# One launch of a four-layer graph transformer: two more norms tile by tile, a sixth region for expert weights, second norm statistics on ScalarE

## What is computed

```python
# layer 0, feed-forward: 64 soft-slot experts, one slot each
x = x + _L0_ffn_ref(_layernorm(x), phi, scale, w1, b1, w2, b2)      # w1 64x768x192, w2 64x192x768, combine at the end
xn = _layernorm(x)                                                  # "combine norm"
# layer 1: graph part with the edge counts as adjacency and degrees; attention from xn
x = x + _L1_gnn_ref(xn, edge_index, W, b) + _L1_mix_ref(xn, kqv_w, ...)
# layer 2, feed-forward
x = x + gelu(x @ mlp_w1 + mlp_b1) @ mlp_w2 + mlp_b2
xm = _ln(x, ln2_g, ln2_b)                                           # "mlp norm"
logits = xm @ gate_w.T + gate_b                                     # router, top 2 of 4 experts
# layer 3, attention projection, then the router and 8 experts
y = xn + x_attn @ W_proj + b_proj
x = x + gnn + (y - mean(y)) * rsqrt(var(y) + eps) * gamma + beta
logits = x @ Wg
```

## Time and profile before

| | |
|---|---|
| median of 3 runs | 2898.76 us (2897.23 to 2898.79) |
| the profiled execution | 2899.39 us, its span 2897.3 us |
| PE busy | 2711.2 us, 94% of the span |
| DVE, ACT, POOL busy | 49%, 39%, 24% |
| PE waiting for expert weights of layer 0 (`w1`, `w2`) | 29.5 us in 11 waits, 20.3 us in 13 waits |
| PE waiting for `norm` of a `LinearNorm` | 14.5 us in 6 waits, 7.7 us the longest |
| PE waiting for `norm` of the last projection | 7.3 us, once |

### The profile page before, as it was taken

The page is one execution under the profiler, slowest core; times in us unless marked ns, Lnnn a source line. Parts: engine busy times, 40 slices in busy tenths (PEclk is TensorE's granted clock), DMA queues, the critical chain, the costliest instruction groups (busy, mean ns, idle before and its releaser), DMA issues. The chain is left out here.

```text
span 2897.3 us, 49066 instructions
## 1 busy us (share of the span) xinstructions
PE 2711.2 (94%) x20003; PEld 2467.0 (85%) x20003; DVE 1418.9 (49%) x3603; ACT 1128.7 (39%) x2103; POOL 706.7 (24%) x261
## 2 busy tenths in 40 slices
PE   9999999998678999998899999999998999999899
PEld 9999999995337988998897999999668897797699
DVE  9777465664104135548752552241665563303743
ACT  7633255561003212327731253332563432356331
POOL 0144311110002331220224433323303431113032
PEclk9999999998898999999999999999999999999999
DMA  2022221015992211221021122222001221111022
GB/s 66 12 77 80 88 72 39 29 50 223 413 380 70 71 44 34 66 86 47 12 77 45 60 77 77 68 75 77 28 1 39 67 66 49 44 34 34 23 66 71
DMA packets 164572, 220.08 MB, mean 76 GB/s; under 512 B 21801, under 2 KB 144325, under 8 KB 164350
## 3 DMA queue, kind: packets, MB, share of 16 engines
q1 hardware_dynamic: 164350, 216.95, 22.6%
HBM read 215.00 MB, written 1.92 MB: 75 GB/s over the span
## 5 line engine op out<-in xcount | busy, mean ns | idle before, releaser
L58 PE MATMUL ps<-weights_r,buf_r 128*125 128x256 f32 (+3 forms) x4110 | 545.7, 285 | 5.8 <-DVE kv L2830 1.7
L279 POOL TENSOR_TENSOR weights_r<-weights,head_weights_r 128x1536 fp32r<-128x1536 f32 (+2 forms) x80 | 276.2, 3453 | 1040.2 <-ACT head_weights_r L272 1007.8
L58 PEld LDWEIGHTS ps<-weights_r,buf_r 128*125 128x125 f32 (+1 forms) x4110 | 516.3, 187 | 9.1 <-issue 4.2
L279 POOL TENSOR_TENSOR weights_r<-weights,weights_r 128x1536 fp32r<-128x1536 f32 x76 | 269.5, 3545 | 974.0 <-ACT weights_r L272 974.0
L58 PE MATMUL ps<-xT_r,weights_r 128*128 128x376 f32 (+4 forms) x2028 | 333.8, 309 | 0.0
L58 PE MATMUL ps<-head_weights_r,buf_r 128*125 128x256 f32 (+2 forms) x2250 | 309.8, 284 | 0.0
L58 PEld LDWEIGHTS ps<-xT_r,weights_r 128*128 128x128 f32 (+1 forms) x2028 | 303.2, 189 | 3.2 <-issue 2.2
L58 PEld LDWEIGHTS ps<-head_weights_r,buf_r 128*125 128x125 f32 x2250 | 287.5, 188 | 0.0
L58 PE MATMUL ps<-weights_r,xT_r 128*125 128x256 f32 x1680 | 233.4, 282 | 8.2 <-issue 4.8
L58 PEld LDWEIGHTS ps<-weights_r,xT_r 128*125 128x125 f32 x1680 | 212.9, 186 | 10.6 <-issue 5.4
L272 ACT ACTIVATE head_weights_r<-weights 128x1536 fp32r<-128x1536 f32 (+2 forms) x80 | 114.8, 1435 | 254.7 <-PE ps L58 134.5
(11 more groups left out here) (383 smaller groups left out, 4322.1 us busy)
## 6 DMA issues: line engine op xcount, KB each, us to landing
expert_regions<-in_L_ffn_w SPq DMA_DIRECT2D x64, 576.0 KB, 15.1
expert_regions<-in_L_ffn_w SPq DMA_DIRECT2D x48, 768.0 KB, 20.5
weights<-in_L_mix_fc_w SPq DMA_DIRECT2D x24, 768.0 KB, 4.5
weights<-in_L_gnn_W SPq DMA_DIRECT2D x18, 768.0 KB, 4.6
weights<-in_L_ffn_W SPq DMA_DIRECT2D x12, 768.0 KB, 4.7
weights<-in_L_mix_w_mapT SPq DMA_DIRECT2D x9, 768.0 KB, 5.0
weights<-in_L_gnn_W_out SPq DMA_DIRECT2D x9, 768.0 KB, 4.6
weights<-in_L_mix_kqv_wT SPq DMA_DIRECT2D x9, 768.0 KB, 4.6
```

Source lines behind the costliest of these rows:

```text
L58: mm = net.nc.tensor.matmul(ps, net.r(stationary(s, k)), net.r(moving(m, k)), start=(n == 0 and k == 0), stop=(stop and n == 2 and k == kc ...
L279: self.nc.gpsimd.tensor_tensor(self.r(load.dst), load.dst, self.r(load.high), ALU.subtract).then_inc(self.low_made, 1)
```

## The change

1. `SlotExperts.DEPTH` becomes 6. The sixth region lies over the edge counts and the mask, with 1568 further columns. `KeepCounts` writes the counts to DRAM early, its stores stand on SP; the region's first load waits for them and for the last graph attention of layer 0, and SP loads the counts back during the layer 1 queries, for `Degrees`, which moves behind `Square`, and `Apply`.
2. The combine norm and the mlp norm become `PairedNorm`, tile by tile over their two units; the low parts of tiles 0 to 3 go to POOL (`lows="gpsimd"`), which cannot read PSUM: without columns ACT first copies the transposes to SBUF. The last tile's transposes are issued behind the next stage's first product (`prior=normed`).
3. In every `PairedNorm` the last unit's `split_high` on ACT stands ahead of the last tile's work instead of behind it, and so POOL's `split_low` of it can start earlier.
4. In `LinearResidualNorm` tiles 0 to 3 get the second statistics from ACT: a pass that sums the row, `centre`, a pass that sums squares, `root2`. `inverse2`, `shift` and ACT's `norm` of a tile come one product later; the last tile keeps the old way. Its transposes are issued in the router.

The core of the diff:

```diff
-        sizes = dict(xT=BUF, ..., weights=(WSLOTS + 1) * SLOT)
+        sizes = dict(xT=BUF, ..., weights=(WSLOTS + 1) * SLOT, edges=NT * N + 3 + 1568)
+        self.expert_blocks = ... + [blocks(1152, ("edges", 0, 4))]
+        self.tile_blocks = ... + [blocks(1536, ("edges", 0, 3))]
@@ LinearT.tensor
             if self.tiles is not None and (j == 0 or part == 0):
-                pe.wait_ge(*self.tiles[2 if self.prior and j == 0 else 3 if j == 0 else 4])
+                for t in (2,) if self.prior and j == 0 else (3,) if j == 0 else (3, 4):
+                    pe.wait_ge(*self.tiles[t])
@@ PairedNorm.__init__
+        self.copied = lows == "gpsimd" and not columns
+        changes = lambda t: 3 if columns else int(self.copied and t < last)
+        lowered = lambda t: [("low", t, g) for g in halves] if lows == "vector" else []
+        for i in range(pair):
+            pe.append(("product", i))
+            dve += [("add", i), ("moments", i)]
         for t in range(NT):
-            pe.append(("product", t))
-            dve += [("add", t), ("moments", t)]
-        for t in range(NT):
-            turned = [("low", t - 2, g) for g in halves] if t > 1 else []
-            pe += [("product", NT + t), ("product", 2 * NT + t)] + [("turn", t - 1, g) for g in halves if t > 0]
+            turned = lowered(t - 2) if t > 1 else []
+            pe += [("product", pair + t), ("product", pair + NT + t)] + [("turn", t - 1, g) for g in halves if t > 0]
             ...
             if t > 0:
                 act += [q for g in halves for q in columned(t - 1, g)]
+                pool += [("low", t - 1)] if lows == "gpsimd" else []
+        dve += lowered(last - 1)
+        if self.weights:
+            act.append(("weights", len(self.weights) - 1))
         if columns:
             act += columned(last, 0)
             dve += columned(last, 1) + [("low", last, 1), ("low", last, 0)]
         else:
             ...
-        act.append(("weights", 2))
@@ PairedNorm.gpsimd
+        for load in self.weights[1:2]:
+            self.net.split_low(load.unit + 2, load.segment)
+        for _, t in self.order["pool"]:
+            ...
+            self.wait(pool, "act", "high", t, 1)
+            self.nc.gpsimd.tensor_tensor(self.net.r(lo), lo, self.net.r(hi), ALU.subtract).then_inc(...)
+        for load in self.weights[2:] or self.weights[:1]:
             self.net.split_low(load.unit + 2, load.segment)
@@ LinearResidualNorm.__init__
-                if n == 0 and t > 0:
+                if n == 1 and t > 0:
                     dve += [("inverse2", t - 1), ("shift", t - 1)]
                     act += [("norm", t - 1)] + [("high", t - 2, g) for g in range(2) if t > 1]
-            dve += [("inverse", t), ("scaled", t), ("sum", t), ("stats", t, 0), ("stats", t, 1), ("mean2", t)]
-            act += [("root", t), ("root2", t)]
+            dve += [("inverse", t), ("scaled", t), ("sum", t)]
+            act += [("root", t)] + ([("total", t), ("centre", t), ("squares", t), ("root2", t)] if t < NT - 1 else [])
+        dve += [("stats", last, 0), ("stats", last, 1), ("mean2", last)]
@@ SlotExperts
-    EXPERTS, GROUP, DEPTH, TILES = 64, 4, 5, 3
+    EXPERTS, GROUP, DEPTH, TILES = 64, 4, 6, 3
@@ network
+    KeepCounts(net, loops.ends())
+            FirstFetches(net, ins["L0_ffn_w1"], (5,), attended + [(net.kept, 32)])
-    normed = LinearNorm(net, units[0]["xT"], units, R, tok(G[2]), XT, 1e-5)
+    normed = PairedNorm(net, units[0]["xT"], units, R, tok(G[2]), XT, 1e-5, lows="gpsimd")
-    degrees = Degrees(net, rdeg)
-    made = linear_T(net, XT, w, feat(G[0]), ..., tiles=normed.made)
+    made = linear_T(net, XT, w, feat(G[0]), ..., tiles=normed.made, prior=normed)
+    counts = net.into(None, None, second.ends()[:1])
+    counts.value, counts.before.used_at = 16 * len(counts.pieces), (queries, 2)
+    degrees = Degrees(net, rdeg, counts, start)
-    normed = linear_norm(net, hT, ins["L2_ffn_mlp_w2"], X, tok(G[0]), XT, 1e-5, ..., kp=96, ...)
-    scored = router(net, XT, ins["L2_ffn_gate_wT"], ..., tiles=normed.made)
+    normed = paired_norm(net, hT, ins["L2_ffn_mlp_w2"], X, tok(G[0]), XT, 1e-5, ..., kp=96, ..., lows="gpsimd")
+    scored = router(net, XT, ins["L2_ffn_gate_wT"], ..., tiles=normed.made, prior=normed)
-    scored = router(net, XT, ins["L3_ffn_Wg"], logits, tiles=normed.made)
+    scored = router(net, XT, ins["L3_ffn_Wg"], logits, tiles=normed.made, prior=normed)
```

More of the change, by code:

```diff
@@ L1128, with __init__ @@
 class PairedNorm(LinearNorm):
-    def __init__(self, net, xT, units, x, out, outT, eps, columns=None, first=None, after=None, tiles=None):
+    def __init__(self, net, xT, units, x, out, outT, eps, columns=None, first=None, after=None, tiles=None, lows="vector"):
         Stage.__init__(self, net, after)
-        self.xT, self.units, self.tiles = xT, units, tiles
+        self.xT, self.units, self.tiles, self.lows = xT, units, tiles, lows
         self.x, self.out, self.outT, self.eps, self.columns, self.first = x, out, outT, eps, columns, first
@@ new lines, in __init__ @@
+        pe, act, dve, pool = (self.order[e] for e in ("pe", "act", "dve", "pool"))
+        last, halves, pair = NT - 1, (0, 1), NT * (len(units) - 2)
+        self.weights = [load for load in dict.fromkeys(u["load"] for u in units) if isinstance(xT, Pair)]
+        self.copied = lows == "gpsimd" and not columns
+        changes = lambda t: 3 if columns else int(self.copied and t < last)
+        columned = lambda t, g: [("column", t, g, c) for c in range(changes(t))] + [("high", t, g)]
+        lowered = lambda t: [("low", t, g) for g in halves] if lows == "vector" else []
@@ L1177, in __init__ @@
                 net.freed[b] = (ticks.sem, self.at[engine]["column", q[1], q[2], 2])
+            elif self.copied and q[1] < last:
+                net.freed[b] = (net.act.sem, self.at["act"][("high",) + q[1:]])
             else:
                 net.freed[b] = (net.dve.sem, self.at["dve"][("low",) + q[1:]])
-        self.made = [(net.dve.sem, self.at["dve"]["low", t, 0 if columns and t == last else 1]) for t in range(NT)]
+        self.made = [(net.pool.sem, self.at["pool"]["low", t]) if ("low", t) in self.at["pool"] else
+                     (net.dve.sem, self.at["dve"]["low", t, 0 if columns and t == last else 1]) for t in range(NT)]
         self.take(**{e: len(seq) for e, seq in counted.items()})
@@ L1345, in __init__ @@
         self.bank = {}
-        for q in pe:
+        for q in pe + list(self.late):
             b = self.bank[q] = net.bank()
@@ L1374, in turn, with turn_last @@
             mm = self.nc.tensor.transpose(self.net.ps[:, b % BANKS, c * TP:(c + 1) * TP], self.out[:, t, (3 * g + c) * 128:(3 * g + c + 1) * 128], self.net.ident[:TP, :TP])
-        mm.then_inc(self.net.pe.sem, self.net.pe.one())
+        mm.then_inc(ticks.sem, ticks.one())
+    def turn_last(self, pe):
+        for g in range(2):
+            self.turn(pe, NT - 1, g, self.net.late)
     def place(self, t, g):
@@ L1446, in scalar @@
                 hi, lo, ps = self.place(t, q[2])
-                self.wait(act, "pe", "turn", t, q[2])
+                if t == NT - 1:
+                    act.wait_ge(self.net.late.sem, self.late["turn", t, q[2]])
+                else:
+                    self.wait(act, "pe", "turn", t, q[2])
                 ins = nc.scalar.activation(hi, ps, ACT.Identity)
@@ L3361, in vector @@
         self.begin(dve)
+        self.landed(dve)
         done = self.net.dve
@@ L3414, in linear, with paired_norm @@
     return Linear(net, xT, units, evac if kind in ("copy", "relu") else "d", rows=[bias] if bias else (), after=after, stats=stats, tiles=tiles, coefs=coefs, prior=prior)
[L3417 to L3419 removed]
+def paired_norm(net, xT, w, x, out, outT, eps, columns=None, first=None, rows=None, kp=128, after=None, tiles=None, lows="vector"):
+    return PairedNorm(net, xT, linear_units(net, w, x, "add", x, rows, kp=kp), x, out, outT, eps, columns, first, after, tiles, lows)
 def linear_norm(net, xT, w, x, out, outT, eps, columns=None, first=None, rows=None, kp=128, after=None, tiles=None, more=None, early=None):
```

110 lines of the change are left out of this document (71 added, 39 removed).

## The result

| | before | changed |
|---|---|---|
| median | 2898.78 us (20 runs, 2894.44 to 2904.46) | 2906.0 us (20 runs, 2899.93 to 2916.29) |
| ratio to before | | 1.0026, 95% interval 1.0017 to 1.0034 |
| the profiled execution | 2899.39 us, span 2897.3 | 2911.05 us, span 2909.3 |

The change makes the kernel 7.2 us slower, 0.26%. The forecast was 2901.9 in a range of 2893.5 to 2907.5. The range holds and so does the direction; the size, 7.2 us for the 3.1 that I had forecast, lies just past the 0.2% within which I had put 0.66 of the chance. The profiled execution lies 5 us above its median, and its span is 12.0 us above before's. So the median is the size to explain, and the trace says where.

The account below looks back on a forecast made before the run. PE is busy 94% of the span, so only its waits count. The terms -5.7 + 1.9 + 5.9 + 2.8 - 0.7 - 0.6 - 0.5 = +3.1 us on the median 2898.76 gave 2901.9, range 2893.5 to 2907.5.

Parts of the forecast that it names:

- Sixth region: Layer 0 expert turns: one more turn is fetched early, so the stream moves one turn of w1 less, -5.7 us.
- Combine norm: Combine norm to queries: POOL holds the first norm, then 3.6 us a tile, low parts on POOL 1.7; queries +1.9 us later.
- Earlier splits: Norms before fc1 and behind fc2: POOL's earlier split holds DVE's low parts, +5.9 us; PE's clock after idling, +2.8.
- Layer 1 router: Norm without columns, nothing collides: ACT can start the split 2.5 us sooner, ending PE's 0.71 idle, -0.7 us.
- mlp norm: mlp norm: the router's first product moves into the gap before the last transposes, -0.6 us, bounds -3 and +1.5.
- Last projection: Last projection: router's first product moves ahead, but POOL's split for the first expert comes 2 us later; -0.5 us.
- No collision: Rival, chance 0.18: the ports do not collide at the two PairedNorm ends, 5.9 and 2.8 fall away, 2893.2 us.
- Lows that hold the norms: Rival, chance 0.19: POOL's low parts hold three norms up to 1.7 us each and the cast is held, 2907.8 us.
- Region without a gain: Rival, chance 0.06: the sixth region gives nothing, as loads are held up or PE's clock bounds turns, 2907.6 us.

Follow-up runs that it names:

- e3: The kernel before with only the sixth region (DEPTH 6, counts kept in DRAM and read back, Degrees moved): 2893.44 us, ratio 0.9983.
- e1: The changed kernel with the last unit's split behind the last tile's work again in every PairedNorm: 2893.13 us, ratio 0.9982.
- e2: The kernel before with only the split moved ahead of the last tile's work, in all four uses of PairedNorm: 2905.39 us, ratio 1.0023.
- e1c: The changed kernel with the split behind the last tile's work only in the norms with columns: 2894.69 us, ratio 0.9985.
- e7: The changed kernel with the split ahead of the last tile's work only in the mlp norm, behind it elsewhere: 2892.67 us, ratio 0.9978.
- e9: e7 with the combine norm as before the change (LinearNorm, low parts by DVE): 2894.59 us, ratio 0.9982.
- e13: The changed kernel with the last tile's second group rounded by ACT instead of DVE's cast, in norms with columns: 2904.56 us, ratio 1.0028.
- e10: e7 with the last projection and its router as before the change: 2893.08 us, ratio 0.9978.
- e8: e7 with ACT taking the combine norm's first root ahead of the high parts of two weight units: 2890.21 us, ratio 0.9965.
- e14: e8 with the combine norm's low parts on DVE and matmuls of zeros on PE in the combine norm alone: 2887.23 us, ratio 0.9957.
- e12: e8 with matmuls of zeros on PE while it waits in the combine norm and the mlp norm: 2889.74 us, ratio 0.9977.

## Why the prediction was right, and where not

- **Sixth region, -5.7.** Right: alone -5.6 (e3). The stretch is 3.8 to 6.1 us shorter in the twelve traces that have the region; in three of the four below 5 the last turn took 5.7 to 5.8 us instead of 4.09, by PE's clock.
- **Combine norm, +1.9.** By the traces 1 to 2. The mechanism was the one named: the first `norm` held by POOL's split, 3.11 us, 3.6 us a tile, POOL's lows 1.78 for 1.7 and just missing the norms.
- **Earlier splits, +5.9 and +2.8.** Right in kind, 8.7 forecast and 10.6 in the trace; e1 and e2 show that the split's place makes both. Two sizes were off. I had let the cast run free, since no row decided; it is the cast that was held, for 3.2 us. The sum would have been nearer with the rule that I had left out of it. The Trainium skill (SBUF — State Buffer, Who interferes with whom) has a cast in a 2-port mode held as well. The trace agrees, 3.6 us for 0.42, and PE's two stops are together 0.8 us longer than I had them. The other is the clock, 1.4 a stop: it was 1.3 at `fc1` and 2.7 at `fc2`, where four groups took 1.5 us instead of 0.87.
- **Layer 1 router, -0.7.** The gain is 0.2 to 0.3 at an equal clock, and no median shows it. The 0.71 idle us in front of the next stage are gone, as I had it. But the step "ACT can start the split 2.5 us sooner" overlooked when the weights land and what the split then delays: ACT waits 0.94 us for them, makes the high parts in front of the last tile's, and PE idles 2.01 instead of 1.34 us before the router's second product. The +2.5 of the profiled execution is the clock (e1c).

```profile
1143.55 1.49 ACT L273 ACTIVATE weights_r<-weights 128x1536 fp32r<-128x1536 f32 x1 [0.94 <-DMA weights<-in_L_ffn_w]
1144.94 0.84 ACT L1318 ACTIVATE xT_r<-ps 128x375 fp32r<-128x375 f32 x2
1146.69 0.85 PE L58 MATMUL ps<-buf_r,head_weights_r 128*8 128x252 f32 x6 [2.01 <-DVE buf_r L1277]
```

- **mlp norm, -0.6.** -2.1, inside the bounds (my own times, 2258.5 and 2257.7, give -0.8 and not -0.6). I had POOL's split end near the last low parts' due time, as it did (the cast was held by 0.3), but had not seen that the split of before holds a subtraction with the router's COPY behind it only if it comes late (e1 against e7). The number is partly luck: with the same order there, the stretch is +1.3 in e9 and +2.5 in e13.
- **Last projection, -0.5.** The number fits, -0.4, by another way. I had POOL's split come 2 us later and hold the next stage; it comes 0.4 later, the router gains 2.7 us by its second product, and the next stage starts 1.9 sooner. What I hadn't followed are the stages behind: all but 0.4 is given back there, most of it to the clock: the first group behind the gates' small matmuls takes 2.23 us at 2783.14 and the next 1.55, and they took 1.29 and 1.20 before. e10 shows no worth of the part in all.
- **The rivals.** No collision: refuted by the cast. Lows that hold the norms: true of two norms in the mlp norm, 0.9 us each, one of them hidden, and of none in the combine norm. Region without a gain: refuted by e3.
- **What the sum left out.** +3.1 was forecast, 7.2 measured; the profiled execution has 12.0. By the table the parts but the router's come to 5.0 of that (-4.5 + 1.4 + 4.6 + 6.0 - 2.1 - 0.4). The rest lies in stretches that the change doesn't touch, or touches by half a microsecond. The largest, 2290 to 2703, is +3.2 in the changed kernel, and within 0.1 of that in e7, e8 and e14, and 0.1 or less in e1, e2 and e3. Half of it lies at one set of 30 transposes that took 3.39 us before:

```profile
2481.81 5.05 PE L1666 MATMUL ps<-ident,buf 125*128 125x125 f32 x30 [1.85 <-issue]
```

The granted clock over the set (2481.8 to 2486.9) was 0.67, 1.00 before. The other half is lost likewise behind 2621.94. Seven traces show the slow set, all with the split ahead in the mlp norm, and seven don't, e9 and e13 among them, which have it ahead too. Why some lose the clock at that place and some don't stays open, and with it about 3 us of what separates the forecast from the profiled execution.

## What to carry to other kernels

Moving a subtraction on POOL a microsecond earlier is no free move: look for which DVE instruction with its data in SBUF starts while it runs, and what PE does meanwhile; decide place by place, since at one place PE's wait fell by 1.9 us and at two the move cost 4.6 and 6.0. Follow a gain through the next stages before booking it: those of the mlp norm and of the last projection were mostly gone a few stages on. And ask what each engine does first behind a long transfer-bound stretch: there a one-column root, moved ahead of two weight conversions, was worth 6.2 us by the trace, as much as the sixth region, though the medians show 2.5 of it.

## What the runs showed of the hardware

- DVE beside a long POOL instruction: a cast of 375 columns took 3.6 us for 0.42, two subtractions 2.36 for 1.01, a `norm` of 768 columns 1.5 to 3.1 for 0.68. An add out of PSUM took 0.54 and statistics of 384 columns 0.56 in the middle of a split (e8), as elsewhere.
- In these rows the engine that starts first isn't held, even by 0.1 us: POOL at 1696.02, DVE at 1696.13, and DVE ends behind POOL. Where POOL came second, a split of 3.45 us took 3.76 (e8: DVE's `norm` from 873.40, POOL from 874.43).
- An idle stop of 3.7 to 3.9 us of PE cost it another 1.3 to 2.7 us at 1.2 GHz, half of 2.4; fillers in place of the stops kept the granted clock at 1.00 over the combine norm (e12, e14; 0.61 in e8), at 0.71 us for one matmul of zeros of 384 columns (two instructions).
- Traces of the same code differ by more than 4 us in a stretch by the clock: the layer 1 router is +2.5 in the changed kernel at a granted clock of 0.65 and -1.9 in e13 at 1.00. The runs of one version lie 3 to 16 us apart. So terms of 1 to 2 us come neither from a stretch's length in one trace nor from these medians; the waits and durations that repeat from trace to trace give them.
